# One convolution block on one core: v kept as pairs of channels by tokens, without a copy for each unit, and x and the networks' weights in v's free half

## Chip, core and metric

The kernel runs on one core of one Trainium2 chip. The metric is the device time of one execution in microseconds (us); less is better. A run's time is somewhat longer than its span, the stretch from the first to the last instruction.

## What is computed

Eight images of 64 by 64 tokens with 96 channels are normalised, projected twice to 288 channels (u and v, each with a silu), v is convolved along rows and along columns with filters that two small networks make, and the sum, gated with u, is projected back and added to the input.

```python
u = silu(srms(x) @ u_w.T + u_b)
v = silu(srms(x) @ v_w.T + v_b)
# a = rpe_net(positions): 4 layers of 256, one filter of 128 positions for each of 288 channels
out = tno(v, along columns, network 2) + tno(v, along rows, network 1)
return (u * out) @ o_w.T + o_b + x
```

A `tno` is, for each channel, a product of 64 tokens with a 64 x 64 Toeplitz matrix of the network's values.

## The kernel before

It works on four images at a time (a half), in 32 steps of 512 tokens; 4 steps are a chunk, 8 channels a unit, and 36 units make the 288 channels. Five stages follow one another, with some overlap: the projections of the first half (phase_a, 0 to 170 us), its convolution (phase_c, to 335), the output of the first half together with the projections of the second (body0, to 545), the second convolution (to 716), and the output of the second half (body1). Each engine has its own program, written by hand, and they meet at semaphores; SP's program issues every DMA, in its order, and each SP wait holds back all DMAs behind it.

- **Projections.** POOL squares x (L417, a chunk in four pieces), DVE sums and inverts the norms, POOL scales a step's x by them (L404) into one of two tiles xa. PE transposes the next step's xa (L937) and then projects the present step in four pairs (L946), first two pairs of v, then two of u; ACT takes the transposed x out of PSUM (L512) and applies the silu (L517), to v in SBUF and to a tile of u, u_out in odd steps and a part of u_in in even ones, that SP stores in DRAM (L264). A silu into such a tile waits for the store two steps back. POOL's order in a chunk c is: scale steps 0 and 1 of c, square piece 0 of chunk c + 2, scale step 2, square piece 1, scale step 3, square pieces 2 and 3.
- **x.** `x_all` holds all eight chunks of the first half at the end of v's place; SP loads chunk c + 3 when phase_a reaches chunk c (L291). v is written over it later.
- **Networks.** In chunks 0 to 3 PE also runs the two networks (L904 to L928) with weights r_lw, r_ow, r_ob, which SP loads at the start (L231 to L235) between the loads of x's chunks 1 and 2; PE waits for all of them ahead of step 0. Their result r_a is stored in DRAM as `a_dram` ahead of chunk 4 (L246).
- **Convolution.** v is [128 partitions, 128 token groups, 288 channels], so one channel of a partition lies at a step of 1152 bytes. For each unit ACT copies v by channels into one of two tiles vc (L564), PE multiplies toepA (loaded as weights) with vc (moving, L1011), transposes v (loaded as weights, L993), and multiplies with toepB (L1024); ACT takes the transposed v out into vt (L572) and the sum back into v (L578). DVE makes toepA and toepB out of staged values (L802), which SP loads (L287).
- **Gate.** POOL multiplies u, read back from DRAM, by the convolved v (L471), a step at a time; PE transposes it (L956) and projects it out (L966, L969), DVE adds x (L857), and SP stores the result (L275), four output buffers in the last stage (L269 waits for the store that last used one).

Of the kernel before, what the change touches and what calls it, by code (L numbers as in the profile page):

```python
# [33 lines left out]
D = 288  # L34
# [24 lines left out]
def tno_kernel(nc, x, x_eT, u_wT, u_b, v_wT, v_b, o_wT, o_b, pos_w, pos_b, lwT, lb, out_wT, out_b, out):  # L59
# [7 lines left out]
    with ctx:  # L67
# [11 lines left out]
        R0 = 79104  # L79
        r_lw = place("r_lw", [P, 2, LAYERS, RC, RPE], R0)  # L80
        r_ow = place("r_ow", [P, 2, RC, D], R0 + 12288)
        r_ob = place("r_ob", [1, 2, D], R0 + 16896)

# [21 lines left out]
        vc = [place(f"vc{k}", [P, UNIT, P], V + (13824, 18432)[k]) for k in range(2)]  # L105
        vt = [place(f"vt{k}", [P, UNIT, P], V + (36864, 45056)[k]) for k in range(2)]

        r_h = place("r_h", [P, 2, RC, P], V + 36864)
        r_sq = place("r_sq", [P, 2, RC, P], V + 38912)
        r_in = place("r_in", [P, 2, RC, P], V + 40960)  # L110
# [7 lines left out]
        r_pw = place("r_pw", [P, 2, 2, RC], V + 18432)  # L118
        r_lb = place("r_lb", [P, 2, LAYERS, RC], V + 18464)
# [58 lines left out]
        vc_ready, vt_transposed, vt_ready = sem("vc_ready"), sem("vt_transposed"), sem("vt_ready")  # L178
        toep_zeroed = sem("toep_zeroed")
        columns_done, conv_done, conv_out = sem("columns_done"), sem("conv_done"), sem("conv_out")  # L180

# [24 lines left out]
        def _(sp):  # L206
# [10 lines left out]
            def load_x_all(c):  # L217
                wait(sp, x_all_loaded, 32 * c)
                for i in range(2):
                    sp.dma_start(x_all[H * i:H * i + H, CH * c:CH * (c + 1)].rearrange("p s n e -> p (s n) e"),  # L220
                                 rows_of(0, CH * c, CH, i)).then_inc(x_all_loaded, 16)
# [4 lines left out]
            sp.dma_start(w_raw[0:E, 0], v_wT).then_inc(weights_loaded, 16)  # L226
            sp.dma_start(w_raw[E:KE, 0], v_b).then_inc(weights_loaded, 16)
            sp.dma_start(w_raw[0:E, 1], u_wT).then_inc(weights_loaded, 16)
            sp.dma_start(w_raw[E:KE, 1], u_b).then_inc(weights_loaded, 16)
            load_x_all(1)  # L230
            sp.dma_start(r_lb[:], lb).then_inc(rpe_loaded, 16)  # L231
            for n in range(2):
                sp.dma_start(r_lw[:, n], lwT[n].rearrange("l (c p) o -> p l c o", p=P)).then_inc(rpe_loaded, 16)
                sp.dma_start(r_ow[:, n], out_wT[n].rearrange("(c p) o -> p c o", p=P)).then_inc(rpe_loaded, 16)
                sp.dma_start(r_ob[0:1, n], out_b[n:n + 1, :]).then_inc(rpe_loaded, 16)  # L235
# [155 lines left out]
        def _(pool):  # L391
# [14 lines left out]
            def scale_a0(t, c, r):  # L406
                pool.wait_ge(norms_ready, c + 1)
                wait(pool, x_transposed, t - 1)
                scale(t, x_all[:, bass.ds(t, 1)].rearrange("p s n e -> p (s n) e"), r)
# [9 lines left out]
            def square_a0(c, r):  # L419

                if r == 0:
                    pool.wait_ge(x_all_loaded, 32 * (c + 1))
                    wait(pool, norms_summed, c)
                square(x_all[:, bass.ds(CH * c + r, 1)].rearrange("p s n e -> p (s n) e"),
                       x_sq[:, NB * r:NB * (r + 1)])
# [10 lines left out]
            def phase_a(c, first, last):  # L436
                for r in range(CH):
# [4 lines left out]
                    if not (isinstance(c, int) and c >= CHUNKS - 2):  # L442

                        for k in ((), (0,), (1,), (2, 3))[r]:
                            square_a0(c + 2, k)
            chunks(pool, phase_a)
# [20 lines left out]
            def gate(half, t, r, loads, start=0, end=D):  # L467

                pool.wait_ge(u_loaded[r % CH], 16 * CHUNKS * half + 16 * loads)
                tile = u_in[:, r % CH, :, start:end]  # L470
                return nc.gpsimd.tensor_tensor(  # L471
                    out=tile, in0=tile, in1=v[:, bass.ds(t * NB, NB), start:end], op=ALU.mult)
# [35 lines left out]
        def _(act):  # L508
# [5 lines left out]
            def silu(xs, pair, target):  # L514
# [611 lines left out]
```

## Time and profile before

| what | us |
|---|---|
| median of three runs | 843.44 |
| lowest and highest run | 840.05, 843.59 |
| the profiled execution | 840.65 |
| its span | 838.6 |
| PE busy | 780.2 (93%) |
| ACT busy | 637.2 (76%) |
| DVE busy | 527.5 (63%) |
| POOL busy | 282.0 (34%) |

The page and the trace come from the profiled execution. Busy shares are means over five stages with different limits, so a stage is read by its own window, and what sets its end by the chain of waits, which is followed back from the last instruction. A timeline row gives start, length, engine, line, operation and, in brackets, how long the engine stood idle before it and what ended that.

### The profile page before, as it was taken

How to read it: one execution, taken by the hardware profiler on the slowest of the kernel's cores; microseconds unless marked ns; L12 is line 12 of the kernel's file. 1: busy time of each engine (PE TensorE's matmuls, PEld its weight loads, DVE VectorE, ACT ScalarE, POOL GpSimd, SP SyncE). 2: the span in 40 equal slices, each digit the busy share in tenths (PEclk: the TensorE clock that was granted, in tenths of full speed). 3: DMA queues.
4: the chain of work that ended last, by engine and by line, in shares of the span. 5: the costliest groups of instructions: out<-in, count | busy, mean ns of one | idle time of the engine just before them, and what ended most of it. 6: DMA issues, size and time to landing. Idle time of an engine off the chain costs nothing.

```text
span 838.6 us, 16989 instructions
## 1 busy us (share of the span) xinstructions
PE 780.2 (93%) x5996; PEld 725.7 (87%) x5996; DVE 527.5 (63%) x917; ACT 637.2 (76%) x794; POOL 282.0 (34%) x191
## 2 busy tenths in 40 slices
PE   0999979999999999899999999989999999897886
PEld 0999879999999999799999999979999999765654
DVE  7666534259999999444554445455655665676666
ACT  0666657789999998777788787769999999665554
POOL 4334332221112112645555454210000001866664
PEclk9999999999999999999999999989999999999999
DMA  9455463497777675688888888685445444777876
GB/s 222 135 158 176 148 164 142 166 222 159 169 167 173 140 162 158 195 279 260 273 268 275 273 262 275 196 199 121 113 120 125 113 116 143 223 250 247 253 249 190
DMA packets 128985, 160.97 MB, mean 192 GB/s; under 512 B 67288, under 2 KB 94108, under 8 KB 128924
## 3 DMA queue, kind: packets, MB, share of 16 engines
q1 hardware_dynamic: 128924, 160.15, 68.2%
q8 instruction: 39, 0.64, 0.3%
q14 instruction: 22, 0.18, 0.1%
HBM read 109.49 MB, written 50.63 MB: 191 GB/s over the span
## 4 chain that ended last, share of the span: by engine, by line
PE 80%; DMA 12%; DVE 2%; ACT 1%; issue 1%; SPq 1%; POOL 1%; POOLq 0%; ACTq 0%; DVEq 0%
PE ps L946 24%; PE ps L1011 16%; PE ps L1024 15%; DMA out<-x_e 9%; PE ps L993 8%; PE ps L966 6%; PE ps L956 5%; PE ps L937 3%; POOL u_in L471 1%; PE ps L969 1%; SPq L269 1%; DMA u_dram<-u_in 1%; DMA stage<-a_dram 1%; DMA u_in<-u_dram 1%; PE ps L920 1%
## 5 line engine op out<-in xcount | busy, mean ns | idle before, releaser
L471 POOL TENSOR_TENSOR u_in<-u_in,v 128x1152 f32<-128x1152 f32 (+2 forms) x66 | 171.4, 2602 | 191.7 <-DMA u_in<-u_dram 175.8
L564 ACT COPY vc<-v 128x1024 f32<-128x1024 f32 x72 | 170.8, 2372 | 6.3 <-DMA out<-x_e 6.3
L848 DVE TENSOR_TENSOR g<-ps,g 128x512 fp32r<-128x512 f32 (+1 forms) x192 | 125.6, 681 | 73.0 <-ACT g L536 45.7
L1011 PE MATMUL ps<-vc,toepA 128*128 128x128 f32 x1152 | 144.1, 279 | 6.1 <-DVE toepA L802 4.2
L1011 PEld LDWEIGHTS ps<-vc,toepA 128*128 128x128 f32 x1152 | 137.3, 195 | 6.7 <-issue 6.4
L1024 PE MATMUL ps<-toepB,vt 128*128 128x128 f32 x1152 | 140.5, 275 | 0.0
L1024 PEld LDWEIGHTS ps<-toepB,vt 128*128 128x128 f32 x1152 | 134.8, 192 | 0.0
L802 DVE COPY toepA<-stage 64x512 f32<-64x512 f32 x144 | 110.0, 764 | 33.5 <-DMA stage<-a_dram 15.2
L742 DVE TENSOR_TENSOR xl<-ps,xh 96x512 fp32r<-96x512 f32 x64 | 44.0, 687 | 130.4 <-ACT xh L512 130.4
L946 PE MATMUL ps<-wu,xh 97*128 97x288 f32 x512 | 122.8, 305 | 2.4
L946 PE MATMUL ps<-wv,xh 97*128 97x288 f32 x512 | 119.3, 308 | 4.6 <-ACT u_in L517 4.2
L802 DVE COPY toepB<-stage 64x512 f32<-64x512 f32 x144 | 94.6, 657 | 44.3 <-PE ps L1024 40.5
L956 PE MATMUL ps<-ident,u_in 128*128 128x128 f32 (+1 forms) x768 | 101.7, 276 | 20.6 <-POOL u_in L471 20.5
L956 PEld LDWEIGHTS ps<-ident,u_in 128*128 128x128 f32 (+1 forms) x768 | 81.3, 127 | 35.7 <-POOL u_in L471 13.1
L517 ACT ACTIVATE v<-ps 128x576 f32 (+1 forms) x128 | 83.5, 652 | 35.3 <-PE ps L946 23.3
L532 ACT CAST g<-ps 128x512 fp32r<-128x512 f32 x128 | 68.8, 590 | 48.1 <-PE ps L956 48.1
L966 PE MATMUL ps<-g,wo 128*96 128x512 f32 x384 | 102.8, 403 | 0.0
L946 PEld LDWEIGHTS ps<-wu,xh 97*128 97x128 f32 x512 | 88.3, 188 | 11.5 <-issue 4.0
L517 ACT ACTIVATE u_out<-ps 128x576 f32<-128x576 f32 x96 | 62.6, 652 | 40.9 <-PE ps L946 38.4
L946 PEld LDWEIGHTS ps<-wv,xh 97*128 97x128 f32 x512 | 87.7, 192 | 5.6 <-ACT u_in L517 4.5
L578 ACT COPY v<-ps 128x1024 f32<-128x1024 f32 x72 | 72.9, 1013 | 22.0 <-PE ps L1024 22.0
L993 PE MATMUL ps<-ident,v 128*128 128x128 f32 x576 | 77.1, 278 | 0.0
(75 smaller groups left out, 1004.9 us busy)
## 6 DMA issues: line engine op xcount, KB each, us to landing
stage<-a_dram SPq DMA_DIRECT2D x144, 256.0 KB, 4.2
u_in<-u_dram SPq DMA_DIRECT2D x64, 576.0 KB, 5.3
u_dram<-u_out SPq DMA_DIRECT2D x48, 576.0 KB, 3.3
x_e<-in_x_eT SPq DMA_DIRECT2D x64, 192.0 KB, 3.8
out<-x_e SPq DMA_DIRECT2D x64, 192.0 KB, 3.8
u_dram<-u_in SPq DMA_DIRECT2D x16, 576.0 KB, 2.9
x_all<-in_x SPq DMA_DIRECT2D x16, 384.0 KB, 5.3
x_n<-in_x SPq DMA_DIRECT2D x16, 384.0 KB, 5.4
```

The source lines that it names most:

```text
L471: return nc.gpsimd.tensor_tensor(out=tile, in0=tile, in1=v[:, bass.ds(t * NB, NB), start:end], op=ALU.mult)
L517: nc.scalar.activation(target, ps[:, b:b + 2, 0:D], ACT.Silu).then_inc(silu_done, 1)
L564: nc.scalar.copy(vc[n % 2][:], v[:, :, UNIT * n:UNIT * n + UNIT].rearrange("p m c -> p c m")).then_inc(vc_ready, 1)
L578: nc.scalar.copy(v[:, :, UNIT * n:UNIT * n + UNIT], ps[:, bank:bank + 2].rearrange("p b (c m) -> p m (b c)", m=P)).then_inc(conv_out, 1)
L802: nc.vector.tensor_copy((toepA, toepB)[axis][n % 2][rows, :, rows], stage[n % STAGES][rows, axis].rearrange("p k c -> p c k")[:, :, ::-1]) ...
L848: nc.vector.tensor_tensor(out=low, in0=ps[0:w, bank], in1=high.bitcast(f32), op=ALU.subtract).then_inc(gl_ready, 1)
L946: last = nc.tensor.matmul(ps[:, n, 0:D], (xh, xl)[xp][r % 2][:, n * P:(n + 1) * P], w[:, wp], start=(k == 0), stop=(k == len(SPLIT) - 1))
L956: last = nc.tensor.transpose(columns[:, n // 2, n % 2], u_in[:, r % CH, n, k * P:k * P + KW[k]], ident[:])
L966: nc.tensor.matmul(ps[0:E, bank], wo[:, 2 * k + wp], tile[:, 2 * k + gp], start=(k + s == 0), stop=False)
L993: last = nc.tensor.transpose(ps[:, VT_BANK + c // NB, (c % NB) * P:(c % NB + 1) * P], v[:, :, UNIT * n + c], ident[:])
L1011: last = nc.tensor.matmul(ps[:, SET_BANK[n % 2] + c // NB, (c % NB) * P:(c % NB + 1) * P], toepA[n % 2][:, c], vc[n % 2][:, c], start=(c % ...
L1024: last = nc.tensor.matmul(ps[:, SET_BANK[n % 2] + c // NB, (c % NB) * P:(c % NB + 1) * P], vt[n % 2][:, c], toepB[n % 2][:, c], start=Fals ...
```

## The change

v becomes [128 partitions, 144 pairs of channels, 128 token groups, 2]: the two channels of a pair lie side by side for each token group, and one channel of a partition lies at a step of 8 bytes over 1024 bytes. What wrote or read v follows that order: silu writes 4 elements (two token groups, two channels) at a time, the convolution's sum is written contiguously, the gate reads pairs at a step of 1024 bytes, PE's transpositions load weights at a step of 8 bytes. The copy into vc and its semaphore are gone: PE moves v itself at the step of 8 bytes.

Phase_a fills token groups 0 to 127 of v in order, so the upper half of each pair's 1024 bytes is free until step 16. In these free rows of 512 bytes lie now x's chunks 0 to 3 (in rows of 384 bytes), the networks' weights and tiles, and the raw projection weights, each loaded in rows of at most 512 bytes by more DMAs. x's chunks 4 to 7 lie in three tiles x_late; chunk 7 takes chunk 4's tile, so its load waits until chunk 4 is scaled and is issued at the start of chunk 5 rather than of chunk 4. POOL's phase_a is written out instead of a loop, in the same order.

```diff
-        v = place("v", [P, STEPS * NB, D], 0)
-        w_raw = place("w_raw", [KE, 2, D], 0)
-        x_all = place("x_all", [P, STEPS, NB, E], V_BYTES - STEPS * NB * E * 4)
+        v = place("v", [P, D // 2, STEPS * NB, 2], 0)
+        free_rows = place("free_rows", [P, D // 2, 2, P], 0)
+        def rows(first, count, width=P, partitions=slice(0, P)):
+            return free_rows[partitions, first:first + count, 1, 0:width]
...
+        x_late = [place(f"x_late{k}", [P, CHUNK_ROWS, E], V + offset) for k, offset in enumerate((36864, 13824, 0))]
+        def x_chunk(c):
+            if c < FREE_CHUNKS:
+                return rows(CHUNK_ROWS * c, CHUNK_ROWS, E)
+            return x_late[(c - FREE_CHUNKS) % 3][:]
...
             for n in range(2):
-                sp.dma_start(r_lw[:, n], lwT[n].rearrange("l (c p) o -> p l c o", p=P)).then_inc(rpe_loaded, 16)
-                sp.dma_start(r_ow[:, n], out_wT[n].rearrange("(c p) o -> p c o", p=P)).then_inc(rpe_loaded, 16)
+                for o in range(RC):
+                    sp.dma_start(rows(lw_row(n, o, 0, 0), LAYERS * RC),
+                                 lwT[n].rearrange("l (c p) (o q) -> o p (l c) q", p=P, q=P)[o]).then_inc(rpe_loaded, 16)
+                for c in range(RC):
+                    sp.dma_start(rows(OW + NCH * (RC * n + c), NCH, E),
+                                 out_wT[n, P * c:P * c + P].rearrange("p (h q) -> p h q", h=NCH)).then_inc(rpe_loaded, 16)
...
             def phase_a(c, first, last):
-                if c + 3 < CHUNKS:
+                if c + 3 < CHUNKS - 1:
                     load_x_all(c + 3)
+                elif c + 2 == CHUNKS - 1:
+                    sp.wait_ge(x_scaled, CH * (c + 2 - 2))
+                    load_x_all(c + 2)
...
                 return nc.gpsimd.tensor_tensor(
-                    out=tile, in0=tile, in1=v[:, bass.ds(t * NB, NB), start:end], op=ALU.mult)
+                    out=tile, in0=tile, in1=v[:, start // 2:end // 2, bass.ds(t * NB, NB)].rearrange("p c n e -> p n c e"),
+                    op=ALU.mult)
...
-                silu(STEPS * half + t, pair, v[:, bass.ds(t * NB + 2 * pair, 2)])
+                silu(STEPS * half + t, pair, v[:, :, bass.ds(t * NB + 2 * pair, 2)],
+                     projection(pair).rearrange("p n (c e) -> p c n e", e=2))
...
-                if n >= 2:
-                    act.wait_ge(columns_done, UNITS * half + n - 1)
-                nc.scalar.copy(vc[n % 2][:], v[:, :, UNIT * n:UNIT * n + UNIT].rearrange("p m c -> p c m")
-                     ).then_inc(vc_ready, 1)
...
-                    nc.scalar.copy(v[:, :, UNIT * n:UNIT * n + UNIT],
-                                   ps[:, bank:bank + 2].rearrange("p b (c m) -> p m (b c)", m=P)).then_inc(conv_out, 1)
+                    nc.scalar.copy(v[:, UNIT // 2 * n:UNIT // 2 * (n + 1)],
+                                   ps[:, bank:bank + 2].rearrange("p b (c e m) -> p (b c) m e", e=2, m=P)
+                                   ).then_inc(conv_out, 1)
...
-                                                   v[:, :, UNIT * n + c], ident[:])
+                                                   v[:, UNIT // 2 * n + c // 2, :, c % 2], ident[:])
...
-                    pe.wait_ge(vc_ready, N + 1)
...
-                                                toepA[n % 2][:, c], vc[n % 2][:, c],
+                                                toepA[n % 2][:, c], v[:, UNIT // 2 * n + c // 2, :, c % 2],
```

In SP's queue, from the stores of the networks' result on, before:

```order
L246 DMA a_dram<-r_a 128x36x8 [waits a_ready]
L246 DMA a_dram<-r_a 128x36x8
L220 DMA x_all<-in_x 64x16x96 [waits x_all_loaded]
L220 DMA x_all<-in_x 64x16x96
L264 DMA u_dram<-u_in 128x1152 [waits silu_done]
L264 DMA u_dram<-u_out 128x1152 [waits silu_done]
```

The same place after:

```order
L272 DMA a_dram<-r_a 128x36x8 [waits a_ready]
L272 DMA a_dram<-r_a 128x36x8
L290 DMA u_dram<-u_in 128x1152 [waits silu_done]
L290 DMA u_dram<-u_out 128x1152 [waits silu_done]
L290 DMA u_dram<-u_in 128x1152 [waits silu_done]
L290 DMA u_dram<-u_out 128x1152 [waits silu_done]
L242 DMA x_late_64<-in_x 64x16x96 [waits x_all_loaded,x_scaled]
L242 DMA x_late_64<-in_x 64x16x96
```

The two loads of x's chunk 7 moved from ahead of chunk 4's four stores of u to behind them.

On POOL, inside the loop over chunks 1 to 5 (L417 squares a piece of the chunk after next, L404 scales a step), before:

```order
L404 TENSOR_TENSOR xa_63<-x_all,rn 128x384
L422 ISA
L186 REGISTER_ALU [waits x_all_loaded]
L417 ISA [waits norms_summed]
L417 TENSOR_TENSOR x_sq<-x_all 128x384
L404 ISA [waits x_transposed,norms_ready]
L404 REGISTER_ALU
L404 TENSOR_TENSOR xa_62<-x_all,rn 128x384
```

In chunk 5 after (L434 scales, L447 squares):

```order
L434 TENSOR_TENSOR xa_59<-x_late_65,rn 128x384 [waits x_transposed,norms_ready]
L447 TENSOR_TENSOR x_sq<-x_late_64 128x384 [waits norms_summed,x_all_loaded]
L434 TENSOR_TENSOR xa_58<-x_late_65,rn 128x384 [waits x_transposed,norms_ready]
L447 TENSOR_TENSOR x_sq<-x_late_64 128x384
L434 TENSOR_TENSOR xa_59<-x_late_65,rn 128x384 [waits x_transposed,norms_ready]
```

The order of squares and scalings stays; the square of chunk 7 stands between the scalings of steps 21 and 22, as it did.

On ACT, at the first units of the first convolution (L564 the copy, L572 vt, L578 the sum), before:

```order
L517 ACTIVATE u_out<-ps 128x576 [waits projected,ua_stored1] x2
L564 COPY vc_76<-v 128x1024 [waits silu_done]
L572 COPY vt_78<-ps 128x1024 [waits vt_transposed]
L564 COPY vc_77<-v 128x1024
L572 COPY vt_79<-ps 128x1024 [waits vt_transposed]
L578 COPY v<-ps 128x128x8 [waits conv_done]
L564 COPY vc_76<-v 128x1024 [waits columns_done]
```

After (L589 vt, L595 the sum):

```order
L546 ACTIVATE u_out<-ps 128x576 [waits projected,ua_stored1] x2
L589 COPY vt_75<-ps 128x1024 [waits vt_transposed]
L589 COPY vt_76<-ps 128x1024 [waits vt_transposed]
L595 COPY v<-ps 128x1024 [waits conv_done]
L589 COPY vt_75<-ps 128x1024 [waits conv_done,vt_transposed]
```

The copies into vc are gone (72 rows of ACT), and vt follows the last silu of u at once. PE's order is the same row for row, without the wait for vc.

## Rows read from the trace of the kernel before

**Rows 1.** windows by stage, core 0: length, busy of each engine, PEclk, DMA share, GB/s

```profile
123.00:170.00 47.00, 46.41 (x336) 43.53 (x334) 17.44 (x47) 36.60 (x61) 11.97 (x18) 1.00 0.46 164
172.00:174.00 2.00, 1.98 (x11) 2.00 (x12) 1.70 (x3) 2.00 (x2) 0.00 (x0) 0.59 0.36 142
176.40:335.00 158.60, 158.60 (x1417) 158.32 (x1416) 145.09 (x260) 145.89 (x106) 27.91 (x11) 1.00 0.72 164
716.00:838.00 122.00, 100.48 (x608) 75.25 (x608) 85.39 (x129) 68.09 (x129) 82.61 (x32) 0.99 0.76 236
```

**Rows 2.** chain that ended last, first half's convolution: start us, length, what

```profile
172.02 3.45 PE ps L1011 x16
...
178.34 1.79 PE ps L1011 x16
...
187.27 1.79 PE ps L1011 x16
```

**Rows 3.** groups by line, whole span: count, busy us, mean ns, idle before

```profile
L564 ACT COPY vc<-v 128x1024 f32<-128x1024 f32 x72 | 170.8, 2372 | 6.3 <-DMA out<-x_e 6.3
L471 POOL TENSOR_TENSOR u_in<-u_in,v 128x1152 f32<-128x1152 f32 x62 | 165.3, 2669 | 31.3 <-DMA u_in<-u_dram 31.2
...
L578 ACT COPY v<-ps 128x1024 f32<-128x1024 f32 x72 | 72.9, 1013 | 22.0 <-PE ps L1024 22.0
```

**Rows 4.** timeline, projections on PE: start us, length, engine, line, operation

```profile
156.02 0.29 PE L946 MATMUL ps<-wu,xl 97*128 97x288 f32 x1
...
156.15 0.42 PE L946 MATMUL ps<-wu,xh 97*128 97x288 f32 x2
```

**Rows 5.** timeline, start of the first convolution, with idle before

```profile
169.47 1.60 DVE L802 COPY toepA<-stage 64x512 f32<-64x512 f32 x2 [4.50 <-DMA stage<-a_dram]
169.91 1.97 ACT L564 COPY vc<-v 128x1024 f32<-128x1024 f32 x1
...
184.47 1.95 DVE L802 COPY toepA<-stage 64x512 f32<-64x512 f32 x2 [3.44 <-DMA stage<-a_dram]
```

**Rows 6.** timeline of SP's queue, projections' fourth and fifth chunk

```profile
102.15 4.11 SPq L246 DMA_DIRECT2D a_dram<-r_a  x2
106.31 4.13 SPq L220 DMA_DIRECT2D x_all<-in_x  x2
110.48 1.39 SPq L264 DMA_DIRECT2D u_dram<-u_in  x1
...
123.18 0.32 SPq L264 DMA_DIRECT2D u_dram<-u_out  x1
```

**Rows 7.** timeline of PE in the same stretch

```profile
112.67 0.60 PE L937 MATMUL ps<-ident,xa 128*96 128x128 f32 x4
117.49 0.42 PE L946 MATMUL ps<-wv,xh 97*128 97x288 f32 x1 [4.22 <-ACT u_in L517]
...
122.31 0.60 PE L937 MATMUL ps<-ident,xa 128*96 128x128 f32 x4
```

**Rows 8.** DMA issues, 80 to 92 us: KB each, median us to landing

```profile
x_all<-in_x SPq DMA_DIRECT2D x2, 384.0 KB, 5.4
```

**Rows 9.** windows of 1 us at the start

```profile
10.00:11.00 1.00, 0.00 (x0) 0.00 (x0) 0.98 (x1) 0.00 (x0) 0.00 (x0) 1.00 1.30 233
15.00:16.00 1.00, 0.00 (x0) 0.00 (x0) 0.87 (x5) 0.00 (x0) 0.01 (x1) 1.00 1.09 366
```

**Rows 10.** timeline at the start, POOL and PE

```profile
22.83 0.83 POOL L417 TENSOR_TENSOR x_sq<-x_all 128x384 f32<-128x384 f32 x1 [3.00 <-DMA x_all<-in_x]
...
27.86 0.60 PE L937 MATMUL ps<-ident,xa 128*96 128x128 f32 x4
```

**Rows 11.** chain that ended last, last stage

```profile
716.44 3.06 POOL u_in L471 x2
...
734.54 3.62 DMA out<-x_e
...
823.85 2.66 POOL u_in L471
```

More of the change, by code:

```diff
@@ L225, in _ @@
             sp.dma_start(r_pw[:, 1], pos_b).then_inc(pos_loaded, 16)
[L226 to L229, printed above, removed]
+            for n, (weight, bias) in enumerate(((v_wT, v_b), (u_wT, u_b))):
+                for array, partitions in ((weight, slice(0, E)), (bias, slice(E, KE))):
+                    sp.dma_start(rows(W_RAW + NCH * n, NCH, E, partitions), array.rearrange("p (h q) -> p h q", h=NCH)
+                                 ).then_inc(weights_loaded, 16)
             load_x_all(1)
@@ L441, in phase_a @@
                         square_a0(1, CH - 1)
-                    if not (isinstance(c, int) and c >= CHUNKS - 2):
+                    if c < CHUNKS - 2:
                         for k in ((), (0,), (1,), (2, 3))[r]:
                             square_a0(c + 2, k)
-            chunks(pool, phase_a)
+            for c in range(CHUNKS):
+                phase_a(c, c == 0, c == CHUNKS - 1)
             def zero(tile, count):
@@ L512, in high_x, with silu, projection @@
                 nc.scalar.copy(xh[r % 2][0:E], ps[0:E, bank]).then_inc(xh_ready, 1)
-            def silu(xs, pair, target):
+            def silu(xs, pair, target, source):
                 act.wait_ge(projected, PAIRS * xs + (pair + 1))
-                b = 2 * (pair % 2)
-                nc.scalar.activation(target, ps[:, b:b + 2, 0:D], ACT.Silu).then_inc(silu_done, 1)
+                nc.scalar.activation(target, source, ACT.Silu).then_inc(silu_done, 1)
+            def projection(pair):
+                return ps[:, 2 * (pair % 2):2 * (pair % 2) + 2, 0:D]
             def silu_v(half, t, pair):
@@ L549, in _ @@
             chunks(act, phase_a)
-            def by_channels(half, n):
-                if n == 0:
-                    act.wait_ge(silu_done, PAIRS * STEPS * (half + 1) - 2)
-                if n < 2 and half:
-                    if n == 0:
-                        act.wait_ge(y_transposed, NCH * STEPS)
-                    else:
-                        for k in range(2):
-                            act.wait_ge(o_stored[0][k], 16 * (STEPS // 2))
-                if n >= 2:
-                    act.wait_ge(columns_done, UNITS * half + n - 1)
-                nc.scalar.copy(vc[n % 2][:], v[:, :, UNIT * n:UNIT * n + UNIT].rearrange("p m c -> p c m")
-                     ).then_inc(vc_ready, 1)
             def phase_c(half):
@@ L586, in phase_c @@
                     if n + 1 < UNITS:
-                        by_channels(half, n + 1)
                         evacuate_vt(n + 1)
@@ L713, in rpe_square @@
             def rpe_square():
-                nc.vector.tensor_tensor(out=r_sq[:], in0=r_h[:], in1=r_h[:], op=ALU.mult).then_inc(rpe_squared, 1)
+                nc.vector.tensor_tensor(out=rows(RSQ, 2 * RC), in0=rows(RH, 2 * RC), in1=rows(RH, 2 * RC), op=ALU.mult
+                                        ).then_inc(rpe_squared, 1)
             def rpe_norm(layer):
@@ L750, in _ @@
             for n, w in enumerate((wv, wu)):
-                nc.vector.tensor_copy(w[:, 0], w_raw[:, n]).then_inc(w_split, 1)
+                raw = rows(W_RAW + NCH * n, NCH, E, slice(0, KE))
+                high, low = (w[:, k].rearrange("p (h q) -> p h q", h=NCH) for k in range(2))
+                nc.vector.tensor_copy(high, raw).then_inc(w_split, 1)
                 dve.wait_ge(w_split, 2 * n + 1)
-                nc.vector.tensor_tensor(out=w[:, 1], in0=w_raw[:, n], in1=w[:, 0].bitcast(f32), op=ALU.subtract
-                                        ).then_inc(w_split, 1)
+                nc.vector.tensor_tensor(out=low, in0=raw, in1=high.bitcast(f32), op=ALU.subtract).then_inc(w_split, 1)
             low_x(0, 0)
```

56 lines of the change are left out of this document (30 added, 26 removed).

## The prediction

> **What bounds the kernel now.** First the windows by stage [rows 1]: TensorE is busy in 158.6 of 158.6 us of the first convolution, 46.4 of 47.0 us of the steady projections, and 100.5 of 122.0 us of the last stage. The chain of waits says the same: the convolution's own matmuls follow one another, and the columns' matmuls of unit 1 and unit 3 start at 178.34 and 187.27, so a unit takes 4.465 us of PE and nothing else [rows 2]. The groups by line [rows 3] then give what the change touches. ACT's copy of a unit into vc takes 2372 ns, 72 times, 170.8 us in all: the largest sum of ACT, and yet ACT is busy only 145.9 of those 158.6 us [rows 1], behind PE. So removing it frees an engine that isn't late. I look for the time elsewhere: at the few places where PE does stand still, and at what the moved buffers do to them. The last stage is not PE's: its chain is one landing of the output's store after another, 3.62 us a piece [rows 11], 122.0/32 = 3.81 us a step.
>
> **The steady convolution, 0.** 1152 instructions of 128 columns run at 1.79/16 = 112 ns each, with vc read contiguously [rows 2]. Afterwards the same instructions read v at a step of 8 bytes, 128 columns out of 1024 bytes. No row shows TensorE's moving operand at a step. The nearest is the projections' pace: instructions of 288 columns, contiguous, start 0.13 us apart [rows 4], so that port already delivers 1152 bytes in 130 ns. Even if it had to pass over the unused half, 1024 bytes in 112 ns is about the same rate (9.1 against 8.9 bytes/ns). The other end is ACT's read of v at a step of 1152 bytes, 2372 ns against 1013 ns for the same 1024 elements out of PSUM [rows 3], a factor of 2.3. I take 0, and keep the other end as a rival. What ACT gives back (72 x 2.37 us) is hidden under PE and is worth 0 in the steady part. The Trainium skill, SBUF — State Buffer, section Specifications (TRN2), has lines of 16 bytes that want at least two hits each for full bandwidth; by it a step of 8 bytes costs nothing and a step of 1152 bytes does, which fits ACT's two rows; for TensorE no run here shows it.
>
> **The start of the first convolution, -0.8.** PE's first columns wait for vc, ready at 169.91 + 1.97 = 171.88. Without it the next late thing is toepA, ready at 169.47 + 1.60 = 171.07 [rows 5]: 0.81 us. PE then runs its first 16 instructions in 3.45 us instead of 1.79 [rows 2], at a granted clock of 0.59 in that stretch [rows 1], between the two levels of 1.2 and 2.4 GHz. A shorter gap may spare up to 1.66 us of that, so -2.5 at best. But unit 3 holds it back: its toepA waits for a stage load and is ready at 184.47 + 1.95 = 186.42 [rows 5], while PE takes it at 187.27 [rows 2]. That load is issued by SP's queue and isn't moved, so at most 0.85 us survives, and I take 0.8. The second convolution starts on a stage load too and gives 0.
>
> **The store of the networks' result, -4.9.** In the fourth chunk of projections (steps 16 to 19) SP's queue holds, in this order, the two stores of a (4.11 us), the two loads of x for chunk 7 (4.13 us), and at 110.48 the store of step 16's u [rows 6]. ACT needs that u buffer back, PE needs ACT, and PE stands 4.22 us; step 19 lasts from 112.67 to 122.31, 9.64 us instead of 47.0/12 = 3.92 [rows 1, 7]. The loss is 5.72 us: 4.22 idle and 1.5 in instructions that start slower after it. The change takes those two loads out of this place. The store of u can then be issued when the stores of a are, at 106.3, up to 4.2 us earlier, and lands when ACT is nearly free for it. I leave 0.8 us of the loss: -4.9, ends -3.5 and -5.7.
>
> **The load that is now late, +6.5.** The loads of chunk 7 now stand in SP's queue behind all stores of chunk 4, since their buffer still holds chunk 4. Without the old stall, step 20 begins at 112.67 + 3.92 = 116.6. SP issues step 19's store 123.18 - 122.31 = 0.87 us into the step [rows 6, 7], then the two loads, at 117.8 and, an allowance of mine, 0.8 later. A load lands 5.4 us after its issue [rows 8]: 124.0. POOL meets the first square of chunk 7 between the scalings of steps 21 and 22, waits there for both loads, and has the scaling of step 22 queued behind it: 0.83 us for the square [rows 10], as much for the scaling, 125.7. PE transposes step 22's x ahead of step 21's projections, at 116.6 + 3.92 = 120.5. So PE stands 5.2 us; with the slow instructions afterwards, 1.5 as above, 6.7. I take 6.5, ends 4.0 (a quick landing, no slow instructions) and 8.2 (a landing 1.5 us later). The stores of step 20 and later stand behind the load on SP; the first of them waits for its silu until a step later anyway. Before, the same square found its data there.
>
> **The start, +0.5.** The networks' weights come in rows of 512 and 384 bytes instead of 1024 and 1152. DMA moved 366 GB/s while the long rows ran and 233 while x's rows of 384 bytes ran [rows 9]. 2.16 MB at 366 are 5.9 us; at 233, 9.3: between 0 and +3.4 us, an estimate of 2.7 for the mixture. Behind them in the queue is x's chunk 2. It is squared at 22.83; after two operations of 0.83 PE's transposition of step 2 could start at 24.5, and starts at 27.86 [rows 10]: 3.4 us of cover. PE's wait for all network weights ahead of step 0 has less cover that I can see, so +0.5, ends 0 and +2.5.
>
> **The gate on POOL, +0.5.** It takes 2669 ns contiguous [rows 3]; now v comes in pairs of 8 bytes, 1024 bytes apart. No row has such a read on POOL. Ends: 0, and ACT's price for a strided element, (2372 - 1013)/1024 = 1.33 ns, times 1152 = 1.5 us. Near 0 since half of the elements follow their neighbour; I take 0.2 us. It lies on the chain where stages begin and end (3.06 us and 2.66 us [rows 11]), some 2.3 gates: +0.5, ends 0 and +3.5. Inside the last stage 3.81 - 2.67 = 1.14 us a step cover it.
>
> **ACT's writes of v, 0.** The evacuations already read PSUM at a step and write runs of 32 bytes at 1013 ns; now runs are contiguous. silu writes runs of 16 bytes. Its cover in a projection step is 3.92 - 36.6/12 = 0.87 us [rows 1].
>
> **Sum.** -0.8 - 4.9 + 6.5 + 0.5 + 0.5 = +1.8 us on the profiled execution's 840.65 (a span of 838.6 and 2.05 around it): 842.4. The three timed runs have a mean of 842.36, 1.7 above that execution, so I forecast 844, beside a median of 843.44.
>
> **Rivals.** (1) TensorE's moving read at a step of 8 bytes is slower than 112 ns. Any excess decides at once, for PE has no cover there: 1.15 us per ns. A quarter more gives +32 us, 876; ACT's factor of 2.3 gives +165, 1009. Against it, the rate of rows 4; for it, that no row shows it. 9%. (2) silu's runs of 16 bytes cost as ACT's strided read does: 576 x 1.33 = 0.77 us, twice a step, 0.66 beyond the cover, x32 = +21 in the first projections alone: 865. 5%. (3) The gate pays the full 1.5 us: 4.2 us a step in the last stage, 0.4 beyond 3.81, x32 = +12, and 3.5 on the chain: 859. It decides from 1.14 us a gate. The Trainium skill, GPSIMD Engine Reference, section Performance pitfalls for Q7 kernels, speaks against the change here: reads at a step above 8 bytes cost about one cycle more per element; if the jump between pairs counts as such, its figures give an estimate of 1.0 us a gate, and the sum would be 846. No run of before shows it. 8%. (4) The late load is covered after all, because POOL or the queue runs further ahead than I read: then only -4.9 - 0.8 + 1.0 is left, 837.7. Against it stands SP's order. 10%. (5) That the copies are not gone is excluded by ACT's order: 72 rows fewer.
>
> **How the numbers follow.** The forecast's own case has 68%; its ends, not all at once, are 838 and 852. Half a per cent, 4.2 us, is about what a measurement of this kernel can tell from no change. Slower by more: the first three rivals (22%, less the mild end of the third) and the upper end of the own case (14%), 35%. Faster by more: most of the fourth rival and the lowest end, 10%. Same: 55%. The range of 8 in 10 takes in the fourth rival's 837 and goes up to 854, where the milder gates end; the first two rivals stay out.
>
> **What would show it.** Right: 1.79 us for 16 column instructions; no PE gap near 113 us, one of some 5 us about 7 us later, on POOL's scaling behind a square that waits for x; the gate near 2.7 to 2.9 us; ACT idle in the convolution; the last stage at 3.8 us a step. Wrong: a unit above 4.47 us, a silu above 1.0 us, a gate above 3.8 us, or no gap in the fifth chunk.

## The result, and the profile after

The changed kernel takes 852.89 us (median of four runs, 850.67 to 853.42) against 842.98 us of the kernel before: a ratio of 1.0121, 95% interval 1.0098 to 1.0144. It is slower by 1.2%, some 10 us. The forecast was 844 us; the range, to 854 us, holds the result, but "within 0.5%" was the likeliest case and "slower" came. The profiled execution took 853.42 us, with a span of 851.6 us against 838.6.

The windows by stage of the kernel after (length, busy of PE, PEld, DVE, ACT, POOL, granted clock, DMA share, GB/s), beside [rows 1]:

```profile
123.00:170.00 47.00, 41.35 (x288) 39.09 (x287) 14.21 (x39) 31.47 (x52) 13.40 (x18) 0.93 0.41 143
...
176.40:335.00 158.60, 156.92 (x1371) 156.40 (x1370) 143.28 (x260) 70.09 (x70) 29.81 (x15) 1.00 0.74 170
```

ACT fell from 145.9 to 70.1 us in the first convolution, as meant, and nobody waited for it. But TensorE, busy for 156.92 of the 158.60 us, got through 1371 instructions in that window instead of 1417 (the convolution starts later, but it is also slower), and in the projections from 123 to 170 us it stands still for 5.65 us, where it stood for 0.59 before. So there are two places to look at, and a third, smaller one comes below.

**The convolution.** The chain of waits, one unit in the steady part (start, length, what; L1028 is the columns, L1011 the transposition of v, L1041 the rows):

```profile
198.60 1.82 PE ps L1028 x16
200.42 0.95 PE ps L1011 x8
201.37 1.79 PE ps L1041 x16
```

A unit takes 1.82 + 0.95 + 1.79 = 4.56 us; before, it took 4.465 [rows 2]. Over 72 units the 0.095 us are 6.8 us. The rows, whose operands weren't touched, take 1.79 us as ever. The groups by line of the kernel after (count, busy us, mean ns, idle before):

```profile
L500 POOL TENSOR_TENSOR u_in<-u_in,v 128x1152 f32<-128x1152 f32 x62 | 168.4, 2721 | 29.3 <-DMA u_in<-u_dram 29.3
L1011 PEld LDWEIGHTS ps<-ident,v 128*128 128x128 f32 x576 | 74.5, 206 | 0.0
```

and the transposition's weight load in the kernel before:

```profile
L993 PEld LDWEIGHTS ps<-ident,v 128*128 128x128 f32 x576 | 71.3, 192 | 0.0
```

The gate on POOL costs 2721 ns instead of 2669 [rows 3], ACT's evacuation of the sum takes 1013 ns as it did, and the transposition's weight load, which now reads v at a step of 8 bytes instead of 1152, went from 192 to 206 ns.

**The queue in the projections.** SP's queue in the fourth and fifth chunk of the kernel after, beside [rows 6]:

```profile
103.30 5.16 SPq L272 DMA_DIRECT2D a_dram<-r_a  x2
108.50 3.47 SPq L290 DMA_DIRECT2D u_dram<-u_in  x1
...
123.56 0.32 SPq L290 DMA_DIRECT2D u_dram<-u_out  x1
124.00 1.60 SPq L242 DMA_DIRECT2D x_late<-in_x  x2
```

The chain of waits runs through that store of u, which lands 7.41 us after its issue, at 115.91. First this line, then the same store in the chain of the kernel before, where it landed at 116.68:

```profile
108.50 7.41 DMA u_dram<-u_in
```

```profile
110.48 6.20 DMA u_dram<-u_in
```

PE in the same stretch (start, length, the idle time ahead of it and who ended it), beside [rows 7]:

```profile
113.81 0.60 PE L955 MATMUL ps<-ident,xa 128*96 128x128 f32 x4
116.72 0.61 PE L964 MATMUL ps<-wv,xh 97*128 97x288 f32 x1 [2.31 <-ACT u_in L546]
...
122.64 0.88 PE L955 MATMUL ps<-ident,xa 128*96 128x128 f32 x4
...
132.27 1.09 PE L955 MATMUL ps<-ident,xa 128*96 128x128 f32 x4 [5.26 <-POOL xa L434]
...
138.00 0.60 PE L955 MATMUL ps<-ident,xa 128*96 128x128 f32 x4
```

L955 opens a step with the transposition of the next step's x: step 19 at 113.81, step 20 at 122.64, step 21 at 132.27. The stall of step 19 is still there though the two loads of x are gone from in front of it: 122.64 - 113.81 = 8.83 us, 4.9 above the normal 3.92. And step 20 takes 9.63 us, step 21 5.73 (the expectation of the first run below calls them 21 and 22): 7.5 us lost on the late load. POOL shows whom the second one waits for:

```profile
130.61 0.83 POOL L447 TENSOR_TENSOR x_sq<-x_late 128x384 f32<-128x384 f32 x1 [18.90 <-DMA x_late<-in_x]
131.39 0.83 POOL L434 TENSOR_TENSOR xa<-x_late,rn 128x384 f32<-128x384 f32 x1
```

Part of each loss comes after the wait: the windows behind the two stalls have a granted clock of 0.50, the lower of TensorE's two levels (1.2 GHz), with PE busy throughout, after it had stood for 2.31 and 5.26 us:

```profile
116.80:122.60 5.80, 5.80 (x24) 5.80 (x25) 2.35 (x2) 2.83 (x5) 0.00 (x0) 0.50 0.25 102
...
133.00:136.50 3.50, 3.50 (x16) 3.50 (x15) 2.23 (x7) 1.36 (x3) 2.36 (x4) 0.50 0.00 0
```

**The steps with the networks.** In nine profiled executions of the new layout (this kernel and the eight variants of it below) the stretch from the opening of step 3 to that of step 15 takes 58.5 to 58.6 us, in the two of the old layout 57.1: 1.4 us, some 0.5 in each of steps 6, 10 and 14. There PE waits for DVE's r_diag, a tile of the networks: at step 6 the products with it start 0.82 us into the step instead of 0.44. DVE and POOL at step 6, after:

```profile
50.02 1.12 DVE L705 TENSOR_SCALAR r_diag<-ident,n_tmp 128x128 f32<-128x128 f32 x2
50.03 0.83 POOL L434 TENSOR_TENSOR xa<-free_rows,rn 128x384 f32<-128x384 f32 x1 [3.08 <-DVE rn L690]
```

and before:

```profile
50.28 0.48 DVE L689 TENSOR_SCALAR r_diag<-ident,n_tmp 128x128 f32<-128x128 f32 x2
50.52 0.92 POOL L404 TENSOR_TENSOR xa<-x_all,rn 128x384 f32 x1 [3.25 <-DVE rn L674]
```

POOL's scaling, no longer in a loop, now starts 0.01 us behind DVE's pair instead of 0.24, and the pair takes 1.12 us instead of 0.48. That the two hold each other up is read from these rows; no run tested it.

The theory to be tested: the difference is the late load (7.5) and TensorE's reads of v at 8 bytes (6.8, the most of it in the transposition's weight load), less what is gained at the first convolution's start; the stall of step 19 is caused by the two stores of a and almost untouched by the change. With the 1.4 us of the networks' steps, 0.8 less at step 19 and 1.9 gained at that start (from the first transposition of v to the last rows 165.22 us instead of 163.74, where 36 units at 0.095 ask for 3.4 more), this makes 13.0 us. So far apart are the two profiled executions (851.6 - 838.6); the medians are 10 apart, mainly because the profiled execution of the kernel before is 2.3 us below its median.

### The profile page after: what moved, and what is told of

It is laid out like the page before. It is cut to its first block, busy times and chain, and to the rows that moved or that the text cites. A ratio compares the mean times of both kernels' runs of the same rounds, so it can differ in the third digit from the quotient of the medians.

```text
span 851.6 us, 16840 instructions
## 1 busy us (share of the span) xinstructions
PE 786.9 (92%) x5996; PEld 731.2 (86%) x5996; DVE 521.0 (61%) x917; ACT 480.8 (56%) x722; POOL 284.5 (33%) x191
## 4 chain that ended last, share of the span: by engine, by line
PE 76%; DMA 13%; DVE 3%; issue 3%; SPq 2%; POOL 2%; ACT 1%; POOLq 0%; ACTq 0%; DVEq 0%
PE ps L964 21%; PE ps L1028 15%; PE ps L1041 14%; DMA out<-x_e 8%; PE ps L1011 7%; PE ps L984 6%; PE ps L974 6%; PE ps L955 3%; DMA stage<-a_dram 2%; DMA u_dram<-u_in 2%; PE ps L987 1%; POOL u_in L500 1%; SPq L295 1%; DMA u_in<-u_dram 1%; PE ps L938 1%
## 5 line engine op out<-in xcount | busy, mean ns | idle before, releaser
L500 POOL TENSOR_TENSOR u_in<-u_in,v 128x1152 f32<-128x1152 f32 (+2 forms) x66 | 174.8, 2653 | 198.2 <-DMA u_in<-u_dram 178.0
L866 DVE TENSOR_TENSOR g<-ps,g 128x512 fp32r<-128x512 f32 (+1 forms) x192 | 125.6, 681 | 73.5 <-ACT g L569 45.2
L1028 PE MATMUL ps<-v,toepA 128*128 128x128 f32 x1152 | 145.1, 277 | 7.4 <-DVE toepA L820 7.4
L589 ACT COPY vt<-ps 128x1024 f32<-128x1024 f32 x72 | 72.9, 1013 | 134.0 <-PE ps L1011 134.0
L1028 PEld LDWEIGHTS ps<-v,toepA 128*128 128x128 f32 x1152 | 138.0, 190 | 8.1 <-issue 5.9
L1041 PE MATMUL ps<-toepB,vt 128*128 128x128 f32 x1152 | 140.4, 275 | 0.0
L1041 PEld LDWEIGHTS ps<-toepB,vt 128*128 128x128 f32 x1152 | 135.1, 193 | 0.0
L595 ACT COPY v<-ps 128x1024 f32<-128x1024 f32 x72 | 72.9, 1013 | 58.0 <-PE ps L1041 58.0
L1011 PE MATMUL ps<-ident,v 128*128 128x128 f32 x576 | 80.0, 282 | 0.0
```

Source lines behind the costliest of these rows:

```text
L500: return nc.gpsimd.tensor_tensor(out=tile, in0=tile, in1=v[:, start // 2:end // 2, bass.ds(t * NB, NB)].rearrange("p c n e -> p n c e"), o ...
L589: nc.scalar.copy(vt[n % 2][:], ps[:, VT_BANK:VT_BANK + 2].rearrange("p b (c m) -> p (b c) m", m=P)).then_inc(vt_ready, 1)
L595: nc.scalar.copy(v[:, UNIT // 2 * n:UNIT // 2 * (n + 1)], ps[:, bank:bank + 2].rearrange("p b (c e m) -> p (b c) m e", e=2, m=P)).then_inc ...
L866: nc.vector.tensor_tensor(out=low, in0=ps[0:w, bank], in1=high.bitcast(f32), op=ALU.subtract).then_inc(gl_ready, 1)
L1011: last = nc.tensor.transpose(ps[:, VT_BANK + c // NB, (c % NB) * P:(c % NB + 1) * P], v[:, UNIT // 2 * n + c // 2, :, c % 2], ident[:])
L1028: last = nc.tensor.matmul(ps[:, SET_BANK[n % 2] + c // NB, (c % NB) * P:(c % NB + 1) * P], toepA[n % 2][:, c], v[:, UNIT // 2 * n + c // 2 ...
```

## Experiments on the queue

Four kernels, each with one or both of two edits. The first puts chunk 7's loads of x behind the store of step 17:

```diff
-                elif c + 2 == CHUNKS - 1:
-                    sp.wait_ge(x_scaled, CH * (c + 2 - 2))
-                    load_x_all(c + 2)
                 for r in range(CH):
+                    if c + 3 == CHUNKS - 1 and r == 2:
+                        sp.wait_ge(x_scaled, CH * (c + 1))
+                        load_x_all(c + 3)
```

The second cuts the stores of a into four and spreads them over chunk 5 (both waits for a_stored then ask for 64):

```diff
-                if c == LAYERS + 1:
-                    store_a()
...
                     store_u(0, CH * c + r, u_tile(0, r), ua_stored[r % 2])
+                    if c == LAYERS + 2:
+                        store_a(r)
```

The early load alone, in the changed kernel:

> The changed kernel with one edit: SP issues chunk 7's two loads of x two steps earlier, behind the store of step 17's u instead of behind all four stores of chunk 4 (their buffer is free when step 19 has been scaled, and that has happened by then). Theory (the load that is late is worth 7.5 us: step 21 lasts 9.63 and the next one 5.73 us instead of 3.92 each): PE's gap of 5.26 us in front of the transposition of step 22 is gone, steps 21 and 22 take 3.92 us each, 845 to 847 us against 853. The stall at step 19, behind the two stores of a, stays at some 5 us. Rival (the queue is only late elsewhere: the loads now hold the stores of steps 18 and 19, and PE loses the same time waiting for their buffers): no less than 851 us, with a new gap of PE behind ACT in steps 18 to 21.

The spread stores alone, in the changed kernel:

> The changed kernel with one other edit: the two stores of a (256 rows of 36 pieces of 32 bytes) are cut into four and issued one by one behind the stores of u of steps 20 to 23, instead of both ahead of step 16's. Theory (the packets of a, not the loads of x, hold the store of step 16's u until 116 us): the stall of some 4.9 us in step 19 goes, the late load keeps its gap of 5 to 7.5 us two steps later, 847 to 850 us against 853. Rival (what held step 16's store before was the loads of x, as the prediction had it, and the rest of the stall has another cause, such as ACT being late): step 19 stays above 8 us, 852 us or more.

Both:

> Both edits in the changed kernel: chunk 7's loads behind step 17's store, the stores of a in four pieces behind those of steps 20 to 23. Theory (two separate losses of 4.9 and 7.5 us): every step of chunks 4 to 7 takes 3.92 us, 840 to 842.5 us; what is left above the kernel before without its own stall is the convolutions' 6.8 us. Rival (one stall in two guises, and the second edit finds nothing left): within 1.5 us of the better of the two single edits, 845 or more.

The spread stores in the kernel before:

> The kernel before with the stores of a in four pieces behind the stores of u of steps 20 to 23; its loads of x for chunk 7 stay ahead of step 16's store. Theory (the stores of a cause the whole loss of 5.72 us at step 19, since the same loads of x do no harm in chunks 1 to 3): 837 to 838.5 us against 843, and step 19 takes 3.92 us. The prediction's reading (the loads of x, 4.13 us in SP's queue, cause 4.9 of it): 841 to 843 us, and step 19 stays above 7 us.

| kernel | median us | ratio to before (95%) | first transposition of v begins on PE at |
|---|---|---|---|
| before, beside these runs | 842.53 | 1 | 169.09 |
| after | 852.89 | 1.0121 (1.0098 to 1.0144) | 176.83 |
| after, early load | 844.11 | 1.0018 (1.0001 to 1.0035) | 169.57 |
| after, spread stores | 847.77 | 1.0070 (1.0053 to 1.0086) | 171.84 |
| after, both | 841.43 | 0.9990 (0.9979 to 1.0002) | 164.21 |
| before, spread stores | 835.88 | 0.9916 (0.9899 to 0.9932) | 164.07 |

The last column is read from each profiled execution and holds everything up to the end of the projections. The early load alone came out below the 845 to 847 us that were expected, and the kernel before with spread stores below its 837 to 838.5; the other two lie in their ranges. At the first transposition of v the two losses add up: the early load brings the transposition forward by 7.26 us alone and by 7.63 with the other edit; the spread stores by 4.99 and by 5.36. (The medians of the whole say it less cleanly: -8.8, -5.1 and -11.5. The runs of the first edit alone scatter from 841.95 to 848.5 us. Its profiled execution is the longest of them: behind the last rows of the second convolution it takes 129 us, where the others take 125 to 126. Why, its trace didn't settle.) With both edits the changed kernel and the kernel before with its stores spread stand 0.14 us apart at this point (in the kernels of both edits further down it is 164.2 to 165.0): up to there the change costs the late load and at most another microsecond, with the networks' steps in it. In the run of the early load alone step 19 and the next take 6.91 and 5.60 us, 4.7 too much together, and those behind them 3.91 and 3.92: the stall of the stores stays, the late load's gap is gone.

PE in the kernel with the spread stores alone has step 19 at its normal length (113.97 to 117.89) and the late load's gap where it was, some five microseconds earlier:

```profile
113.97 0.60 PE L957 MATMUL ps<-ident,xa 128*96 128x128 f32 x4
117.89 0.60 PE L957 MATMUL ps<-ident,xa 128*96 128x128 f32 x4
127.50 1.08 PE L957 MATMUL ps<-ident,xa 128*96 128x128 f32 x4 [5.53 <-POOL xa L436]
```

The fourth kernel decides what held the store of u. SP's queue in the kernel before with spread stores; its loads of x stand where they always stood:

```profile
102.85 1.67 SPq L220 DMA_DIRECT2D x_all<-in_x  x2
106.41 0.33 SPq L266 DMA_DIRECT2D u_dram<-u_in  x1
...
122.44 0.43 SPq L247 DMA_DIRECT2D a_dram<-r_a  x1
```

The same two loads are issued in 1.67 us, not 4.13 [rows 6], and the store behind them in 0.33 us, not 1.39. Their 4.13 us were themselves time in which the queue was held by the stores of a. The DMA issues of the kernel after (100 to 118 us), and of the kernel before with spread stores (120 to 136 us), with KB each and median us to landing:

```profile
a_dram<-r_a SPq DMA_DIRECT2D x2, 144.0 KB, 9.5
```

```profile
a_dram<-r_a SPq DMA_DIRECT2D x4, 72.0 KB, 4.6
```

A store of a goes out in pieces of 32 bytes, and 144 KB of it take 9.5 us to land, against 5.4 us for 384 KB of x [rows 8]. Windows of the kernel after, while the stores of a drained and while that of u did (the last two numbers are the DMA share and GB/s):

```profile
105.50:108.50 3.00, 2.96 (x23) 2.72 (x23) 2.39 (x9) 2.52 (x5) 0.40 (x1) 1.00 0.72 59
113.00:115.50 2.50, 1.41 (x12) 1.15 (x10) 0.00 (x0) 0.00 (x0) 0.00 (x0) 1.00 0.96 376
```

The stores of a keep the DMA engines busy and move little. Two in a row hold all that is issued behind them; one of 72 KB behind each u store finds slack. That the size of the pieces is the reason is argued from these rows: no run stored a in larger pieces.

## Experiments on TensorE's reads

The base is now the kernel with both edits, 841.43 us, whose steps are all 3.92 us. In three kernels TensorE reads v side by side, by a flat view of v:

```diff
+        v_flat = v[:].rearrange("p c m e -> p (c m e)")
...
-    toepA[n % 2][:, c], v[:, UNIT // 2 * n + c // 2, :, c % 2],
+    toepA[n % 2][:, c], v_flat[:, (UNIT * n + c) * P:(UNIT * n + c + 1) * P],
...
-    v[:, UNIT // 2 * n + c // 2, :, c % 2], ident[:])
+    v_flat[:, (UNIT * n + c) * P:(UNIT * n + c + 1) * P], ident[:])
```

The first hunk for the columns alone:

> From here on the base is the kernel of both edits (every step of the projections at 3.92 us, 841.43 us). One edit: the columns' matmuls read their moving operand from 512 bytes side by side of the unit's own v instead of at a step of 8 bytes; the convolution along columns therefore works on other elements than it should, everything else is as it was. Theory (the step of the moving operand costs 113.8 - 111.7 = 2.1 ns per instruction of 128 columns, 1152 instructions): 16 of them take 1.79 instead of 1.82 us, a unit 4.53 instead of 4.56, 2.4 us in all, 839 us. Rival (the unit became longer for another reason, such as ACT's or DVE's traffic at v): a unit stays at 4.56 us, 841 to 842 us.

The second for the transpositions alone:

> The base with the other edit: the transpositions load v as weights from 512 bytes side by side of the unit's own v; the columns' matmuls read at 8 bytes as in the base. The transposed copy therefore holds other elements than it should. Theory (two thirds of the unit's 0.095 us are the weight load at a step of 8 bytes, some 7 to 8 ns for each of 576 transpositions): 8 of them take 0.89 instead of 0.95 us, a unit 4.50, 4.3 us in all, 837 us. Rival (the transpositions are slower because they follow columns that are, and the weight load is hidden): 0.95 us stays, 841 us.

Both:

> Both of these in one: TensorE reads v side by side for columns and transpositions (other elements than it should). Theory (the two prices add up and are all of it): a unit takes 4.465 us as in the kernel before, 6.8 us less than the base, 834 to 835.5 us. Rival (part of the loss is the two accesses together, or other engines): a unit between 4.48 and 4.56 us.

The medians are 839.2 us (ratio 0.9961, 0.9948 to 0.9974), 836.7 us (0.9928, 0.9903 to 0.9954) and 834.81 us (0.9913, 0.9884 to 0.9941). From the base (841.43, 0.9990) these are 2.2, 4.7 and 6.6 us, for 2.4, 4.3 and 6.8 expected. (In these three TensorE reads other elements of v than the convolution needs.) The chain of waits of each, columns and transposition of one unit; first columns side by side:

```profile
641.49 1.79 PE ps L1030 x16
643.28 0.95 PE ps L1013 x8
```

transpositions side by side:

```profile
644.19 1.82 PE ps L1030 x16
646.01 0.87 PE ps L1013 x8
```

both:

```profile
644.45 1.79 PE ps L1030 x16
646.24 0.87 PE ps L1013 x8
```

Each edit repairs its own line and leaves the other as it was, with the other engines' traffic unchanged: there is no common cause, and no need for one in that traffic. A third of the loss is the moving operand, two thirds the weight load. (Side by side the transposition even falls to 0.87 us, below the 0.89 of the kernel before with its step of 1152 bytes. By that a unit of the third kernel is 0.11 us shorter than the base's, 7.9 us in all; 6.6 came out, since PE's waits for toepA at unit 3 of the first convolution and at the start of the second grew from 0.74 and 4.76 us to 1.58 and 5.39.)

The whole price list by step, in one run; for each group of units the edit sets another step for both reads:

```diff
+        STEP = (256,) * 4 + (1,) * 6 + (2,) * 6 + (4,) * 6 + (8,) * 6 + (16,) * 4 + (2,) * 4
+        def v_read(n, c):
+            s = STEP[n]
+            if s == 256:
+                return v_flat[:, 16 * 256 + c:16 * 256 + c + 127 * 256 + 1:256]
+            first = UNIT * n * P + {1: c * P, 2: c // 2 * 2 * P + c % 2, 4: 2 * c, 8: c, 16: c}[s]
+            return v_flat[:, first:first + s * (P - 1) + 1:s]
```

> A look at the price by step, in one run: the base with v read by TensorE at another step in each group of units (other elements than it should): units 0 to 3 at 1024 bytes, 4 to 9 at 4, 10 to 15 at 8, 16 to 21 at 16, 22 to 27 at 32, 28 to 31 at 64, 32 to 35 at 8 bytes. Two theories. A: the price goes with the bytes that are passed over, in lines of some size; it grows with the step up to that size and stays: 8 transpositions 0.95 us at 8 bytes, over 1.0 us at 16 and more, and the columns' 16 instructions above 1.9 us at 32 and 1024 bytes. B: there is a fixed price for anything but 4 bytes, or for 8 bytes alone (the kernel before loaded weights at 1152 bytes for nothing): 0.95 us or less at 16, 32 and 64 bytes too, columns at or below 1.82 us throughout.

Its one run took 908.47 us, since most steps were dear. The chain of waits of its second convolution (L1038 columns, L1021 transpositions), one unit for each step, in order of time 1024, 4, 8, 16, 32 and 64 bytes; for 1024 bytes the transposition stands first:

```profile
594.93 1.12 PE ps L1021 x8
597.84 3.50 PE ps L1038 x16
...
614.87 1.79 PE ps L1038 x16
616.65 0.87 PE ps L1021 x8
...
646.30 1.82 PE ps L1038 x16
648.12 0.95 PE ps L1021 x8
...
670.94 3.65 PE ps L1038 x16
674.60 0.94 PE ps L1021 x8
...
709.22 3.73 PE ps L1038 x16
712.95 0.90 PE ps L1021 x8
...
747.42 3.48 PE ps L1038 x16
750.90 0.90 PE ps L1021 x8
```

For the moving operand theory A holds, in a sharper form than I wrote it: 1.79 us at 4 bytes, 1.82 at 8, and twice that, 3.48 to 3.73, from 16 bytes up to 1024, the largest step of the run. For the weights neither theory holds: 0.87 us at 4 bytes, 0.95 at 8, 0.94 at 16, 0.90 at 32 and 64, 1.12 at 1024, and 0.89 at the 1152 bytes of the kernel before. The price of a weight load goes up and down with the step and stays within 0.25 us per 8; what decides it, these runs don't say. (From 16 bytes on the transpositions also stand behind dear columns, since both reads have the same step; no run set them apart there.) The Trainium skill, SBUF — State Buffer, section Specifications (TRN2), has lines of 16 bytes that need two hits each for full bandwidth; for the moving operand that is where the cliff lies, 1.82 us at two hits a line and 3.65 at one, but at 8 bytes the reads were 2% slower still, and the weight loads don't follow it.

The last run asks the same of POOL and ACT:

```diff
+        v_single = v_flat.rearrange("p (c m) -> p c m", m=P)
...
-    in1=v[:, start // 2:end // 2, bass.ds(t * NB, NB)].rearrange("p c n e -> p n c e"),
+    in1=v_single[:, start:end, bass.ds(t * NB, NB)].rearrange("p c n -> p n c"),
...
+                if half:
+                    silu(STEPS + t, pair, v_single[:, :, bass.ds(t * NB + 2 * pair, 2)],
+                         projection(pair).rearrange("p n c -> p c n"))
```

> How far the prices of POOL and ACT go beyond pairs: the kernel of both edits with TensorE reading v side by side, where in addition the gates of both halves read v one channel at a time (each element 512 bytes from the one before, instead of pairs of 8 bytes 1024 bytes apart) and the second half's silu writes v in runs of 8 bytes instead of 16; both therefore meet other elements than they should. Theory (POOL's and ACT's price for jumps is as small as the 52 ns that pairs cost): the gate stays at 2.7 to 2.8 us, the second half's silu of v at 0.65 us, 834 to 837 us. Rival (the pairs hide a price per element that single elements pay, at most the 1.5 us of the prediction's third rival): a gate of 3.5 to 4.2 us, the last stage's step above 3.81 us, 838 to 850 us.

It took 834.79 us (three runs; ratio 0.9898, 0.9858 to 0.9938), the same as the kernel with both reads side by side, but the rows belie half of the theory. The groups by line of this kernel:

```profile
L503 POOL TENSOR_TENSOR u_in<-u_in,v 128x1152 f32<-128x1152 f32 x62 | 203.0, 3282 | 16.2 <-DMA u_in<-u_dram 16.1
L549 ACT ACTIVATE v<-ps 128x576 f32 x40 | 28.0, 701 | 4.3
```

The first is of the whole span, the second of the second half's projections. Single elements cost the gate 3282 - 2669 = 613 ns, 0.53 ns an element, where pairs cost 52 ns in all; silu pays 49 ns for runs of 8 bytes. Inside the last stage the gate's price is covered, since a step takes 3.81 us [rows 11] and the gate 3.28; silu's is covered too, for the stretch between the convolutions takes 214.5 us in this kernel and in the one with both reads side by side. At the ends of the last stage the gate is on the chain: the last one takes 3.27 us instead of 2.73, the stage opens with 6.92 us of gates instead of 3.11, and from the last rows to the end it takes 128.7 us instead of 125.6. The medians don't show these 3 us; the profiled execution is the longest of the three runs (837.12), and that stretch was as long in the run of the early load without such a gate, so how much of it is the gate stays open. The price was real and for the most part hidden, and the expected time came for another reason than I gave. The Trainium skill, GPSIMD Engine Reference, section Performance pitfalls for Q7 kernels, has half as much again per element for reads at steps above 8 bytes; here single elements cost 23% more and pairs 2%, so the jump between pairs doesn't count as such a step.

## Why the prediction was right and wrong

**Steady convolution: forecast 0, came out at 6.8 us.** Two things failed in this step. It costed one of the two reads that the change alters: the transposition of v takes v as weights, at a step of 1152 bytes before and of 8 after, and no sentence prices it. That is two thirds of the loss. And of the read that it did cost it said 0 where 2.1 ns of 112 were to be paid, 1152 times. The argument by the rate of bytes, that passing over the unused half is nearly free, came close at 8 bytes by luck: by that rate 32 bytes would cost twice what 16 do, and they cost 3.73 us against 3.65. (The row that it leant on also moves parts of x in fp32r, where v is fp32.) A factor of 2, as in the first rival, is real as well: it begins somewhere above 8 bytes and is there at 16. Rival 1 gave 1.15 us per ns; 2.1 ns by that rule is the 2.4 us that the runs show. That the chain had no cover for any excess was read rightly.

**Start of the first convolution: forecast -0.8.** Right for the wait. From the first transposition to the first columns it takes 166.33 - 164.21 = 2.12 us with both queue edits and 167.00 - 164.07 = 2.93 us in the kernel before with spread stores: -0.8, and the columns then wait for toepA:

```profile
166.33 2.06 PE L1029 MATMUL ps<-v,toepA 128*128 128x128 f32 x16 [1.01 <-DVE toepA L821]
```

In the two kernels themselves the gain is larger: the first columns' 3.45 us at a lower clock [rows 1, 2] become 2.06, and unit 3, which waits 1.27 us for its stage's toepA at 193.78, takes part of it back, as the prediction said it would. From the first transposition to unit 3's columns it is 16.95 us instead of 18.02.

**Store of the networks' result: forecast -4.9, came out at about 0.** This is the step that failed most. In [rows 6] the loads of x take 4.13 us in the queue ahead of the late store, and I took that as their own time. It was time in which they, too, stood behind the packets of a. Without the loads the store of u itself was held 3.47 us and landed 7.4 us after its issue, 0.8 us earlier than before; the stall is 4.9 us in place of 5.72, and spreading the stores takes away about 5 us with the loads (164.07 against 169.09) and without them (171.84 against 176.83).

**Late load: forecast +6.5, came out at 7.3 to 7.6 us.** Right in mechanism: gap 5.26 us where 5.2 was worked out, POOL's square waiting with the scaling queued behind it. The slow instructions after it were sized at 1.5; by the trace they are 7.5 - 5.26 = 2.3. The prediction took the old stall to be gone and started step 20 at 116.6; it began at 122.64, and since the load is issued behind step 19's store it moved with the step, so the gap came out as forecast though its place in time didn't.

**Start of the kernel, forecast +0.5; gate, +0.5; ACT's writes, 0.** Up to the opening of step 3 nothing is lost: it comes at 35.5 to 36.4 us in the nine executions of the new layout, at 36.10 and 36.81 in the two of the old. The 1.4 us of the networks' steps behind it are a loss that no term of the sum held. The gate and ACT's writes are small, as said: the gate pays 52 ns where 200 were assumed. silu stays at 652 ns, the evacuation at 1013.

**Sum.** With the stalls of the queue removed from both kernels, the layout alone costs 841.43 - 835.88 = 5.5 us by the medians: 6.6 for TensorE's reads, less the 0.8 at the first convolution's start, within a microsecond, what the networks' steps add included. The two losses of the kernel after are 852.89 - 841.43 = 11.5 us by the medians and 12.6 by PE's rows, the one of the kernel before 842.5 - 835.88 = 6.6 and 5.0: the two ways of reading agree within 1.6 us. The forecast of +1.8 had a gain of 4.9 that isn't there and missed 6.8; that the range held is luck, owed to its upper end, which stood for milder gates, not for this. One of its own signs of being wrong came, a unit of 4.56 us where it named 4.47, and one sign of being right stayed out: PE's gap in step 19 (2.31 us) should have gone. Of the rivals the first came in its mildest form, 2.1 ns an instruction; no gate or silu reached the bound, and the late load wasn't covered.

**A version that beats both** came out of it: the kernel before with its stores of a in four pieces, 835.88 us, 0.8% below the kernel before and 2.0% below the changed one (835.88/852.89). It keeps the copy of each unit's v on ACT, which costs 0.8 us at the first convolution's start and nothing in the steady part.

## What to carry to other kernels

Work taken off an engine that isn't late buys nothing, and what replaces it is paid on the engine that is: when a layout is changed so that a copy can go, price every operand of the full engine that reads the new layout, weights as well as moving ones. Time that an issue spends in a queue is not its own cost: look at what is still draining ahead of it, above all transfers that keep the DMA engines busy and move little, such as these pieces of 32 bytes, and spread those before moving anything else.

## What the hardware showed that I had not expected

TensorE's moving fp32 operand has a cliff between 8 and 16 bytes of step: 16 instructions of 128 columns take 1.79, 1.82, 3.65, 3.73, 3.48 and 3.50 us at 4, 8, 16, 32, 64 and 1024 bytes. Groups of four channels, a step of 16 bytes, would have cost this kernel another 72 x 1.83 = 132 us; 12 bytes weren't run. A weight load isn't monotone in the step: 8 bytes cost 0.95 us for 8 transpositions, 1152 bytes 0.89. And POOL pays 52 ns per 1152 elements for jumps of 1024 bytes between pairs but 613 ns for jumps of 512 bytes between single elements.
